# Third chunk's 1/std by Newton rounds, exponential table and first key early, staircase and words inside the pair loop, fourteen wide tiles

## The reference, cut to what matters

```
# attention, per batch, 16 heads of 8 features; phi(a) = elu(a) + 1
q, k, v = phi(xn @ Wq.T), phi(xn @ Wk.T), xn @ Wv.T
kv    = sum over n of k[n]^T v[n]          # 8 x 8 per head
k_sum = sum over n of k[n]
out   = (q @ kv) / (q . k_sum + 1e-6) @ Wo.T

# experts, 8 of them, one per token
aff    = xn @ centroids.T;  assign = argmax(aff);  alpha = sigmoid(max aff)
order  = argsort(assign)                   # tokens sorted by expert
h      = relu(layernorm(xs) * g[e] + b[e]) @ w1[e].T + b1[e] ...
y      = xs + h @ w2[e].T + b2[e]          # for the rows of expert e
out    = alpha * y + (1 - alpha) * xs      # put back in the old order
```

## Time and profile before

| engine | busy us | share of the span | instructions |
|---|---|---|---|
| PE matmul | 138.0 | 90% | 1138 |
| DVE | 111.8 | 73% | 395 |
| ACT | 101.4 | 66% | 334 |
| POOL | 115.4 | 75% | 137 |

### The profile page before, as it was taken

How to read it: one execution, slowest core, us unless ns; L and a number is a source line. 1 busy time by engine, 2 the same in 40 slices (tenths; PEclk the granted TensorE clock), 3 DMA queues, 4 the chain that set the end, 5 groups by cost and what they waited for, 6 DMA issues and landing times.

```text
span 153.6 us, 4729 instructions
## 1 busy us (share of the span) xinstructions
PE 138.0 (90%) x1138; PEld 131.5 (86%) x1138; DVE 111.8 (73%) x395; ACT 101.4 (66%) x334; POOL 115.4 (75%) x137
## 2 busy tenths in 40 slices
PE   3945999896999999999999999999999999999930
PEld 3945898796988998899999999999999999999920
DVE  3999998999968988897856554667777756556440
ACT  7533988999448786886666657666666666666610
POOL 7644430899958867888887768878888888877774
PEclk9999999999999999999999999999999999999997
DMA  4999200499937999677678998877777777841111
GB/s 142 327 323 420 94 4 0 151 344 294 274 89 214 241 340 286 163 201 192 161 195 233 287 338 205 216 190 207 196 166 174 189 160 174 135 41 53 51 51 51
DMA packets 26601, 29.10 MB, mean 189 GB/s; under 512 B 3024, under 2 KB 20432, under 8 KB 26448
## 3 DMA queue, kind: packets, MB, share of 16 engines
q1 hardware_dynamic: 21808, 23.69, 49.9%
q0 software_dynamic: 4480, 5.05, 17.8%
q10 hardware_dynamic: 288, 0.07, 0.2%
HBM read 18.18 MB, written 10.62 MB: 187 GB/s over the span
## 4 chain that ended last, share of the span: by engine, by line
PE 72%; POOL 9%; DVE 7%; ACT 5%; DMA 3%; issue 2%; SPq 1%; DVEq 0%
PE bank L718 22%; PE bank L706 21%; PE bank L671 6%; POOL out L417 5%; PE bank L688 5%; PE bank L659 4%; POOL feat_k L425 4%; PE bank L596 3%; DVE stats L770 3%; DMA x<-in_x 3%; PE bank L679 3%; PE bank L698 2%; PE bank L651 2%; DVE xn L818 2%; ACT k_exp L510 2%
## 5 line engine op out<-in xcount | busy, mean ns | idle before, releaser
L541 ACT ACTIVATE hT<-bank,b 128x128 f32<-128x128 f32 x156 | 44.6, 369 | 25.8 <-PE bank L706 25.7
L718 PE MATMUL bank<-w,hT 128*128 x312 | 42.8, 280 | 0.8 <-ACT hT L541 0.7
L706 PE MATMUL bank<-zT,feat_k 128*128 128x128 f32 x312 | 41.2, 275 | 0.0
L718 PEld LDWEIGHTS bank<-w,hT 128*128 128x128 f32 x312 | 37.8, 191 | 2.0 <-issue 1.2
L706 PEld LDWEIGHTS bank<-zT,feat_k 128*128 128x128 f32 x312 | 37.9, 192 | 0.0
L409 POOL DMA_INDIRECT out<-rows,token_at x20 | 32.0, 1602 | 6.1 <-issue 6.1
L396 POOL DMA_INDIRECT rows<-z_rows,token_at x20 | 20.6, 1030 | 5.0 <-issue 3.5
L1037 DVE TENSOR_SCALAR zT<-xn,ln_g,ln_b 128x128 f32 x39 | 14.2, 363 | 9.6 <-issue 8.7
L1052 DVE SCALAR_TENSOR_TENSOR rows<-y_own,weight,rows 128x128 f32 x39 | 13.8, 355 | 7.8 <-DVE y_own L1044 5.8
L425 POOL TENSOR_TENSOR feat_k<-feat_k,k_exp 128x256 f32<-128x256 f32 x16 | 14.2, 908 | 7.0 <-ACT k_exp L510 6.4
L396 POOL DMA_INDIRECT rows<-z_base_rows,token_at x12 | 12.0, 1000 | 4.0 <-issue 3.4
(11 more groups left out here) (124 smaller groups left out, 256.9 us busy)
## 6 DMA issues: line engine op xcount, KB each, us to landing
feat_k<-in_w1T SPq DMA_DIRECT2D x39, 256.0 KB, 4.1
z_rows<-xn SPq DMA_DIRECT2D x4, 528.0 KB, 5.0
z_base_rows<-xn SPq DMA_DIRECT2D x8, 264.0 KB, 5.4
x<-in_x SPq DMA_DIRECT2D x8, 256.0 KB, 4.8
w<-in_w2T SPq DMA_DIRECT2D x1, 2048.0 KB, 10.4
out<-x SPq DMA_DIRECT2D x8, 256.0 KB
z_base_rows<-x SPq DMA_DIRECT2D x16, 128.0 KB
b<-in_b SPq DMA_DIRECT2D x1, 512.0 KB, 5.8
```

Source lines behind the costliest of these rows:

```text
L541: last = a.activation(hT[:, par, c * P:(c + 1) * P], bank[hidden_bank(s)][:, c * P:(c + 1) * P], ACT.Relu, bias=b1[:, c, bass.ds(e, 1)])
L706: last = t_.matmul(bank[hidden_bank(s)][:, c * P:(c + 1) * P], w1_now[:, s % W1_RING * FC + c, :], zT[:, s % ZT_RING, :], start=True, stop ...
L718: last = t_.matmul(bank[y_bank(s)][:, 0:D], hT[:, par, c * P:(c + 1) * P], w2[:, bass.ds(e * (FC * D) + c * D, D)], start=(c == 0), stop=( ...
```

## The change

- The third chunk's 1/std and rstd_2 for all tiles are made together on DVE (`rsqrts_of_both`): 12 + 32 columns, an integer guess on the float's bits and three Newton rounds. ACT's square roots of the third chunk and of var_2 go, and `second_norm` shrinks to two instructions.
- ACT loads the exponential table after copy_v(1) and runs exp_of_k(0) there. exp_of_k(1) then stands ahead of the exponential of the affinities.
- `choose` works in parts of 16, 8 and 8 tiles, the second between DVE's copies of pairs 11 and 13.
- PE's ranks go behind keys_values(0). TOKENS_AT goes from 9 to 10.
- On DVE mask_kv(0) goes ahead of hot_lanes(1), mask_kv(1) stays behind hot_lanes(3), slot_tokens comes next. staircase and words leave this place: they run in the pair loop, at the end of j = 1 and of j = 2, and the engines wait for expert_ready at j = 10 (SP still ahead of its first fetch).
- EARLY goes from 20 to 18, so there are fourteen wide tiles instead of twelve, and UNSCATTERED from 27 to 26.

```diff
     EPS_LN, EPS_ATT = 1e-5, 1e-6
+    SEED = float(0x5F3759DF)
+    ROUNDS = 3
     CHUNK = (0, 8, 20, 32)
...
     XN_POOL = 1
-    CHOOSE = (0, 16, 32)
+    CHOOSE = (0, 16, 24, 32)
     V_BY_DVE = (11, 13, 15)
...
     WAKING = 16
-    TOKENS_AT = 9
+    TOKENS_AT = 10
     VALUES_FIRST = 12
...
     SCALE_LAG = 2
-    EARLY = 20
-    UNSCATTERED = 27
+    EARLY = 18
+    UNSCATTERED = 26
     LOOK = 3
...
-            def sqrt_of_second():
-
-                act.wait_ge(var_2_ready, 1)
-                a.activation(std_2[:, :], var_2[:, :], ACT.Sqrt).then_inc(std_2_ready, 1)
-
             def copy_xnT(gr):
...
             expand_lanes(3)
+            def exp_of_k(b):
+
+                part, neg = b % K_BANKS, b % 2
+                act.wait_ge(k_done, b + 1)
+                wait_for(act, k_summed, b - K_BANKS + 1)
+                a.activation(k_neg[:, neg, :], k_bank(b)[:, 0:TB * P], ACT.Relu, scale=-1.0).then_inc(k_neg_ready, 1)
+                a.activation(feat_k[:, TB * b:TB * (b + 1), :].rearrange("p j d -> p (j d)"), k_bank(b)[:, 0:TB * P], ACT.Relu)
+                act.wait_ge(k_neg_ready, b + 1)
+                a.activation(k_exp[:, part, :], k_neg[:, neg, :], ACT.Exp, scale=-1.0).then_inc(k_exp_ready, 1)
+
             copy_xnT(0)
...
             copy_v(1)
+            a.activation(warm[:, :], mean[:, 0:1], ACT.Exp, scale=0.0)
+            exp_of_k(0)
             for gr in range(2, NG + LAG):
...
                         copy_v(b)
-                    if b == 2:
-                        sqrt_of(2)
-                        sqrt_of_second()
-            a.activation(warm[:, :], mean[:, 0:1], ACT.Exp, scale=0.0)
-
-            def exp_of_k(b):
...
-            exp_of_k(0)
+
+            exp_of_k(1)
             act.wait_ge(max_ready, len(CHOOSE) - 1)
             a.activation(alpha_e[:, :], aff_max[:, :], ACT.Exp, scale=-1.0).then_inc(sig_exp, 1)
-            for b in range(1, NB):
+            for b in range(2, NB):
                 exp_of_k(b)
...
             act.wait_ge(bias_in, 16 * 2)
-            act.wait_ge(expert_ready, 1)
             steps = Steps(act)
...
                 if j == WORDS_AT:
+                    act.wait_ge(expert_ready, 1)
                     steps.word(0)
...
                 project_k(b)
-            ranks()
             for b in range(TOKENS_AT + 1):
...
                 keys_values(b)
+                if b == 0:
+                    ranks()
             for b in range(TOKENS_AT + 1 + K_BANKS, NB):
...
                 keys_values(b)
-            pe.wait_ge(expert_ready, 1)
             pe.wait_ge(w2_in, 16)
...
                 if j == WORDS_AT:
+                    pe.wait_ge(expert_ready, 1)
                     steps.word(0)
...
+            def rsqrts_of_both(filling):
+
+                part = slice(CHUNK[NCH - 1], NT)
+                n = NT - CHUNK[NCH - 1]
+                dve.wait_ge(var_ready, NCH)
+                v_.tensor_scalar(raised[:, 0:n], var[:, part], EPS_LN, None, ALU.add)
+                step(v_.tensor_scalar(raised[:, n:n + NT], var[:, :], 1.0 + EPS_LN, EPS_LN * EPS_LN, ALU.mult, ALU.add), filling)
+                v_.tensor_scalar(halved[:, 0:n + NT], raised[:, 0:n + NT], -0.5, None, ALU.mult)
+                step(v_.tensor_scalar(guess[:, 0:n + NT].bitcast(i32), raised[:, 0:n + NT].bitcast(i32), -0.5, SEED, ALU.mult, ALU.add),
+                     filling)
+                for r in range(ROUNDS):
+                    step(v_.tensor_tensor(sq[:, 0:n + NT], guess[:, 0:n + NT], guess[:, 0:n + NT], ALU.mult), filling)
+                    step(v_.tensor_tensor(nw[:, 0:n + NT], sq[:, 0:n + NT], halved[:, 0:n + NT], ALU.mult), filling)
+                    if r < ROUNDS - 1:
+                        step(v_.scalar_tensor_tensor(guess[:, 0:n + NT], nw[:, 0:n + NT], 1.5, guess[:, 0:n + NT], ALU.add, ALU.mult),
+                             filling)
+                v_.scalar_tensor_tensor(rstd[:, part], nw[:, 0:n], 1.5, guess[:, 0:n], ALU.add, ALU.mult).then_inc(rstd_ready, 1)
+                step(v_.scalar_tensor_tensor(rstd_2[:, :], nw[:, n:n + NT], 1.5, guess[:, n:n + NT], ALU.add, ALU.mult), filling)
+                dve.wait_ge(rstd_ready, NCH)
+
             def normalise(c):
...
             moments(2, rows_1, rows_1)
-            next(rows_1)
-            dve.wait_ge(var_ready, NCH)
-            v_.tensor_scalar(var_2[:, :], var[:, :], 1.0 + EPS_LN, EPS_LN * EPS_LN, ALU.mult, ALU.add).then_inc(var_2_ready, 1)
-            rsqrts(2, rows_1)
+            rsqrts_of_both(rows_1)
             finish(rows_1)
...
-                dve.wait_ge(var_2_ready, 1)
-                v_.tensor_scalar(var_2_half[:, :], var_2[:, :], -0.5, None, ALU.mult)
-                v_.scalar_tensor_tensor(spread[:, :], var[:, :], EPS_LN, rstd[:, :], ALU.add, ALU.mult)
-                dve.wait_ge(std_2_ready, 1)
-                step(v_.reciprocal(rough_2[:, :], std_2[:, :]), nothing)
-                step(v_.tensor_tensor(sq_2[:, :], rough_2[:, :], rough_2[:, :], ALU.mult), nothing)
-                step(v_.tensor_tensor(nw_2[:, :], sq_2[:, :], var_2_half[:, :], ALU.mult), nothing)
-                step(v_.scalar_tensor_tensor(rstd_2[:, :], nw_2[:, :], 1.5, rough_2[:, :], ALU.add, ALU.mult), nothing)
+                step(v_.scalar_tensor_tensor(spread[:, :], var[:, :], EPS_LN, rstd[:, :], ALU.add, ALU.mult), nothing)
                 v_.tensor_tensor(xn[:, :, AT_C], spread[:, :], rstd_2[:, :], ALU.mult).then_inc(meta_ready, 1)
...
             choose(0)
+            second_norm()
             copy_v(V_BY_DVE[0])
-            second_norm()
+            choose(1)
             for b in V_BY_DVE[1:]:
                 copy_v(b)
-            for c in range(1, len(CHOOSE) - 1):
-                choose(c)
+            choose(2)
             dve.wait_ge(const_ready, 8)
...
             hot_lanes(0)
+            mask_kv(0)
             hot_lanes(1)
             hot_lanes(2)
-            mask_kv(0)
             hot_lanes(3)
             mask_kv(1)
-            staircase()
+            slot_tokens()
             mask_kv(2)
-            words()
-            slot_tokens()
             mask_kv(3)
...
             dve.wait_ge(bias_in, 16 * 2)
-            dve.wait_ge(expert_ready, 1)
             steps = Steps(dve)
...
                     add_base(s + LOOK + 2)
+                if j == 1:
+                    staircase()
+                if j == 2:
+                    words()
                 if j == WORDS_AT:
+                    dve.wait_ge(expert_ready, 1)
                     steps.word(0)
```

More of the change, by code:

```diff
@@ L124, in linear_attention_and_routed_experts @@
         rstd = sb("rstd", [P, NT])
-        var_2, var_2_half, std_2, rough_2, sq_2, nw_2, rstd_2 = (
-            sb(n, [P, NT]) for n in ("var_2", "var_2_half", "std_2", "rough_2", "sq_2", "nw_2", "rstd_2"))
+        raised, halved, guess, sq, nw = (sb(n, [P, NT + TC]) for n in ("raised", "halved", "guess", "sq", "nw"))
+        rstd_2 = sb("rstd_2", [P, NT])
         spread = sb("spread", [P, NT])
```

25 lines of the change are left out of this document (12 added, 13 removed).

## The result

The changed kernel takes 157.99 us (median of 4 runs, 157.88 to 158.17), the kernel before beside it 155.23 (155.02 to 156.49). The ratio is 1.0162, 95% interval 1.0106 to 1.0217: slower by 2.8 us, where +0.8 was forecast and 157.0 was the range's upper end. The profiled execution took 157.91 us with a span of 156.1.

A forecast was written before the change was run, and what follows sets the result against it. The prediction took POOL's gather and scatter list, anchored at the last zb_out store's landing, as the bound. Front -2.0 and loop +1.5 move the anchor -0.5; the list adds 1.3: +0.8, from 155.09 to 155.9 us, range 154.4 to 157.0.

The forecast's parts named there:

- the anchor: Landing of the last zb_out store, which POOL's first wide gather awaits; forecast to move by -0.5 us.
- front, to num(0): Everything up to the pair loop's first matmul on PE: num(0) at 43.1, 2.0 us earlier.
- loop, num(0) to num(4): First rounds of the pair loop: PE loses 1.5 us waiting for DVE, between 1.3 and 2.2.
- Newton rounds: Third chunk's rstd on DVE: 1.15 us later, of which 1.0 reaches PE and ACT.
- Choose in three and positions: DVE's choice and positions: chosen about 1.0 us later, positions start about 0.45 later, alpha no longer colliding with POOL.
- Masks: mask_kv(0) behind the first lane mask: PE's 1.20 us gap before keys_values(9) goes; num(0) 2.0 us earlier.
- the third rival: The front gives nothing: num(0) at -1.0, loop loss 2.2, anchor +1.2, 157.6 us; chance 0.12.
- Early sums: Early table and first key: POOL's sums come 0.4 to 1.4 us earlier, 0.7 for the middle ones.
- Words in the loop: staircase and words in rounds 1 and 2: DVE price 2.2 us, 0.7 free, PE loses 1.5.
- the first rival: The detour is hidden: DVE's 2.2 us in rounds 1 and 2 cost PE nothing, 154.4 us; chance 0.15.
- the second rival: Stores have landed by 80.5, so idle POOL starts gather 18 1.25 us earlier: 154.65 us; chance 0.15.
- Fourteen wide tiles: POOL's list behind the anchor: two gathers +2.6, two adding scatters made whole -1.3, sum +1.3 us.

The follow-up runs named there:

- c1: Kernel before with the third chunk's rstd and rstd_2 by Newton rounds on DVE, nothing else: 156.85 us, ratio 1.0108.
- c3: Kernel before with choose in three parts (16, 8, 8 tiles) and second_norm ahead of the copies: 156.76 us, ratio 1.0091.
- a4: Changed kernel with the old front (ACT square roots, late table and first key, choose in halves) and twelve wide tiles: 155.43 us, ratio 1.0051 to the kernel before.
- a3: Changed kernel with the old front (ACT square roots, late table and first key, choose in halves), fourteen wide tiles kept: ratio 1.024 to the kernel before, stalling chip.
- c2: Kernel before with Newton rounds, and table load and exp_of_k(0) ahead of copy_xnT(2); choose still in two parts: 158.68 us, ratio 1.0214.
- b1r: Kernel before with fourteen wide tiles alone (EARLY = 18, UNSCATTERED = 26), on a sound chip: 156.50 us, ratio 1.0077.
- d3: Kernel before with SP's w1 fetches held until all z_base_rows stores have landed: ratio 1.0001, stalling chip.
- d1: Kernel before with mask_kv(0) and slot_tokens earlier on DVE, and z_base_rows stores ahead of each piece's out store: ratio 1.002, stalling chip.
- d1r: Kernel before with mask_kv(0) and slot_tokens earlier on DVE, z_base_rows stores ahead of each out store, on a sound chip: 153.94 us, ratio 0.9927.
- d2r: Changed kernel with z_base_rows stores ahead of each piece's out store, on a sound chip: 158.06 us, ratio 1.0203 to the kernel before.
- a1r: Changed kernel with twelve wide tiles again (EARLY = 20, UNSCATTERED = 27), on a sound chip: 157.03 us, ratio 1.0138 to the kernel before.

## Why the prediction was wrong, step by step

The sign was right, and so was the view of the bound: POOL's list behind the anchor sets the end on every chip without the stalls (its last scatter starts 1.2 to 4.3 us behind DVE's last sum, with the usual 0.3 of issue before it). The net of the front failed: of the 2.0 us that it was to give, 0.34 came. In the forecast's own terms, the last scatter against before:

| term | forecast | measured |
|---|---|---|
| front, to num(0) | -2.0 | -0.34 |
| loop, num(0) to num(4) | +1.5 | +1.03 |
| num(4) to the last stores | 0 | +0.56 |
| lag of the landing | 0 | +0.92 |
| POOL's list behind it | +1.3 | +0.78 |
| earlier start of this execution | 0 | -0.45 |
| sum | +0.8 | +2.50 |

*Newton rounds: mis-sized.* 1.15 on DVE and 1.0 on PE were forecast; 1.39 and 1.32 came (c1). Of the slack of 0.15 that I gave PE only 0.07 was there.

*Choose in three and positions: the step that failed.* I wrote that "positions start about 0.45 us later, because alpha no longer collides with POOL". They start 1.94 later, counted from var. Newton alone brings 1.37 (c1), the three parts alone 0.91 (c3); if they are the whole of it, they overlap by 0.34 (ranks behind keys_values(0) gave 0.68 with the old front, a4, and no run takes them alone out of the kernel after). I let the chunk's delay shrink on the way to the scan and took the split choice to be hidden behind copies; c1 and c3 show that neither happens. Alpha did not collide (0.17 where it took 0.69), but token_half, the instruction ahead of it, did in its place: 0.71 in the rows above where it took 0.17. So nothing was won ahead of the scan. Behind it pos_up and lo_neg took 0.76 and 0.74.

*Masks: the gap's cause right, its gain eaten.* From the scan to the end of mask_kv(0) DVE took 37.69 - 27.97 = 9.72 us and takes 36.89 - 29.46 = 7.43: 2.29 saved, 1.94 of it used up. So keys_values(9) still waits 0.92, and from it to num(0) are 7.21 us before and 7.22 after. num(0) at -0.34 net (-0.79 raw) is the third rival's step, "the late third chunk and DVE's later positions eat the mask gap". a3 and a4 bear it out: with the old front PE has no gap there. The rival's time, 157.6, is near the 157.99 for another reason too: its loss of 2.2 in the loop did not come, and the lag stood in for it.

*Early sums: mis-sized, and no gain shown.* 0.7 was taken for the middle ones; counted from var 0.41 came at the ninth. PE's wait at keys_values(9) was for DVE: the tenth sum ended 1.3 us before it. With mask_kv(0) late the early key is harmful (c2); no run takes it out of the kernel after.

*Words in the loop: near in size, and taken to end at num(4).* DVE's price is 1.8 us (forecast 2.2), PE's loss by num(4) 1.03 (1.5). The "rounds have time free" of the first rival is refuted. Behind num(4) I counted nothing, and 0.56 more went: 0.20 by num(15) and 0.36 in the last rounds. The wait for expert_ready, which moved to round 10, is at most part of it. PE does wait 0.51 at num(10) for DVE's heads (0.15 before), but b1r, with words in front, does too; PE of b1r:

```profile
60.74 0.73 PE L671 MATMUL bank<-kv_all,feat_q 128*128 128x144 f32 x4 [0.50 <-DVE heads L1024]
```

Both make most of it up by num(11). From num(4) to num(11) the seven profiles with words in the loop take 11.87 to 12.13 us and the others 11.74 to 11.90; the kernel after has 11.87, before 11.78. The 0.36 of the last rounds is open.

*The anchor.* Forecast -0.5. Stores: - 0.34 + 1.03 + 0.20 + 0.36 = + 1.25; the lag adds 0.92, which I took as fixed. It lay between 2.9 and 5.6 us in the profiles, and the profile before, at 3.32, was a short one. It is set by the last of 32 landings, in the kernel after by two that came 1.1 and 1.5 us behind the rest. Why these parts are late is open: not the w1 fetches (d3), and not the order of the stores alone (d1 2.91, but d1r 4.11 and d2r 4.03). This also answers the second rival, "the stores have landed by 80.5": before, the last landing was at 81.03, so gather 20 did wait for it, as the trace's landings show. A receipt of about 2 us, of which the prediction speaks, does not show: from its "about 80.0" to the last landing are 1.03 us and from there to POOL 0.74, and in d3 the last packets move at 81.4 and the last landing is at 81.95. c3's runs fall into two groups, 155.6 to 156.2 and 157.4 to 158.1; its profile is of the slower group and has the one landing that is 2.04 us late. That the faster group lacks it would fit, but no trace shows that group.

*Fourteen wide tiles.* + 1.3 forecast, + 1.2 alone (b1r), + 0.78 against the long list before, + 1.60 against a1r's. The price holds, and one or two ring waits (0.3 to 0.75 each over the usual gap) come on top, which I took at nothing. a1r's 2.1 us and b1r's 1.2 sum to more than the whole's 2.8, by less than their intervals.

## What to carry to other kernels

A delay at the head of a serial chain arrives undiminished at its end unless a wait on the way is named that takes it up; write the chain down instruction by instruction before letting it shrink. Before two profiles are compared, both are counted from an instruction that the change can't touch. Making one engine's input early won nothing here, and in c2 cost the clock, where another input of the same matmul was the late one. A landing is the last of its parts: over these kernels it moved by 2.7 us, more than most of the effects looked for, so a forecast that leans on one should carry that in its range.
